# Mask phase of a two-layer cross-attention kernel: the crossbar transfers of the probabilities go from ACT's queue to SP's, one for each head

## What is computed

```python
xq = layer_norm(x, qn_w, qn_b); ctx = layer_norm(context, cn_w, cn_b)
q = (xq @ q_w).reshape(B, N, H, D)                       # H = 16 heads of D = 32
k, v = (ctx @ kv_w) split into keys and values
attn = jnp.einsum('bnhd,bmhd->bhnm', q, k) * scale
attn = softmax(jnp.where(xa_mask, neg, attn))
out = jnp.einsum('bhnm,bmhd->bnhd', attn, v).reshape(B, N, C)
x = x + (out @ proj_w + proj_b)
```

## Time and profile before

| | |
|---|---|
| median of 3 runs | 2843.61 us (2843.58 to 2844.65) |
| the profiled execution | 2851.42 us, its span 2849.7 us |
| mean granted TensorE clock in it | 0.974 |
| busy in the span: PE, DVE, ACT, POOL | 2657.4, 2004.7, 1561.3, 935.0 us |
| DMA queue of SP (q1), of ACT (q10) | 201.66 MB, 33.56 MB |

### The profile page before, as it was taken

One profiled execution on the slowest core, in us unless ns is written; L12 is line 12 of the kernel. 1 busy time (PEld: TensorE's weight loads), 2 busy tenths in 40 slices (PEclk: granted clock), 3 DMA queues, 4 the chain that ended last, 5 costly groups with the idle time before them and its releaser, 6 DMA issues.

```text
span 2849.7 us, 67083 instructions
## 1 busy us (share of the span) xinstructions
PE 2657.4 (93%) x23144; PEld 2268.0 (80%) x23144; DVE 2004.7 (70%) x5443; ACT 1561.3 (55%) x4742; POOL 935.0 (33%) x1033
## 2 busy tenths in 40 slices
PE   6888888788789999999999999999999999999997
PEld 5666667666668888888888888888878888888886
DVE  5777777777665344444346888888788888888887
ACT  5656656565552111111125777777766767676764
POOL 4555545455410000000000333333333434343422
PEclk8999999999999999999999999999999999999999
DMA  5545555564542111211122111111232222222210
GB/s 168 131 116 143 124 121 147 120 148 103 139 124 76 45 50 38 59 44 44 59 74 82 45 45 51 44 44 44 91 99 74 81 72 83 71 84 68 87 51 23
DMA packets 313621, 236.11 MB, mean 83 GB/s; under 512 B 150736, under 2 KB 240848, under 8 KB 312656
## 3 DMA queue, kind: packets, MB, share of 16 engines
q1 hardware_dynamic: 180432, 201.66, 22.5%
q10 hardware_dynamic: 133120, 33.56, 7.0%
HBM read 137.65 MB, written 63.96 MB: 71 GB/s over the span
## 4 chain that ended last, share of the span: by engine, by line
PE 71%; ACT 11%; issue 8%; DVE 8%; ACTq 1%; DMA 1%; POOL 0%; DVEq 0%; POOLq 0%
PE cross_work L181 16%; PE mlp_acc L3287 12%; PE mlp_f L3269 12%; PE causal_work L181 9%; ACT mask_prob_even L948 3%; PE cross_scores L2284 3%; ACT mask_prob L948 3%; PE cross_scores L2261 2%; PE cross_attended L2314 2%; PE causal_scores L2284 2%; DVE mask_cT_lo L1486 2%; PE causal_scores L2261 2%; DVE mask_scores L1548 2%; PE causal_attended L2314 1%; PE mask_scores L2261 1%
## 5 line engine op out<-in xcount | busy, mean ns | idle before, releaser
L3062 ACT ACTIVATE mlp_h<-mlp_f,mlp_b1col 128x512 f32<-128x512 f32 x128 | 88.3, 690 | 525.9 <-PE mlp_f L3269 525.9
L3269 PE MATMUL mlp_f<-mlp_xT_hi,mlp_w 128*128 128x512 f32 x1024 | 335.4, 389 | 0.0
L3169 DVE CAST mlp_hT_hi<-mlp_h 128x512 fp32r<-128x512 f32 x128 | 58.2, 454 | 369.9 <-ACT mlp_h L3062 369.7
L3287 PE MATMUL mlp_acc<-mlp_w,mlp_hT_hi 128*128 128x512 f32 x1024 | 315.2, 389 | 0.0
L948 ACT ACTIVATE cross_prob<-cross_scores,cross_low 128x256 f32<-128x256 f32 x512 | 237.1, 490 | 63.6 <-DVE cross_low L1542 63.6
L948 ACT ACTIVATE causal_prob<-causal_scores,causal_low 128x128 f32<-128x128 f32 (+1 forms) x512 | 210.2, 436 | 93.7 <-DVE causal_low L1548 93.7
L1548 DVE CUSTOM_DVE_ANT_0 mask_scores<-mask_scores,mask_mask 128x256 f32<-128x256 f32 x512 | 200.8, 454 | 75.9 <-PE mask_scores L2261 65.8
L3269 PEld LDWEIGHTS mlp_f<-mlp_xT_hi,mlp_w 128*128 128x128 f32 x1024 | 192.2, 188 | 40.5 <-issue 0.4
L3287 PEld LDWEIGHTS mlp_acc<-mlp_w,mlp_hT_hi 128*128 128x128 f32 x1024 | 192.3, 188 | 39.8
L181 PE MATMUL causal_work<-causal_xT_hi,causal_w 128*128 128x256 f32 x1008 | 217.0, 293 | 0.3 <-DVE causal_qk_parts L1498 0.3
L3269 PE MATMUL mlp_f<-mlp_xT_lo,mlp_w 128*128 128x512 f32 x512 | 199.2, 389 | 0.0
(11 more groups left out here) (368 smaller groups left out, 8295.3 us busy)
## 6 DMA issues: line engine op xcount, KB each, us to landing
cross_x_in<-after_attention SPq DMA_DIRECT2D x17, 512.0 KB, 4.1
mask_x_in<-in_x SPq DMA_DIRECT2D x16, 512.0 KB, 5.7
mask_c_in<-in_ctx SPq DMA_DIRECT2D x16, 512.0 KB, 6.6
mask_res<-in_x SPq DMA_DIRECT2D x16, 512.0 KB, 5.5
after_attention<-mask_res SPq DMA_DIRECT2D x16, 512.0 KB, 2.8
mlp_x<-after_attention SPq DMA_DIRECT2D x8, 1024.0 KB, 5.5
mlp_stage<-in_L_xattn_fc_w SPq DMA_DIRECT2D x8, 1024.0 KB, 5.5
after_layer<-mlp_y SPq DMA_DIRECT2D x8, 1024.0 KB, 4.4
```

Of the source, the lines that this page charges most:

```text
L3062: act.activation(h32[:, m % 2, :], F1[m % 2][:], ACT.Gelu, bias=b1col[:, m:m + 1]).then_inc(s["gelu"], 1)
L3269: ins = pe.matmul(F1[m % 2][:], W[2 * (m // 4)][:, a, k, m % 4 * P:(m % 4 + 1) * P], xT[p][:, k, :], start=(k == 0 and n == 0), stop=(k == ...
L3287: ins = pe.matmul(ACC[t][:], hT[a][:, m % 2, t * P:(t + 1) * P], W[2 * (m // 4) + 1][:, p, m % 4, :], start=(m == 0 and n == 0), stop=(m = ...
```

## The change

Each crossed head is a transfer of its own: four of 256 KB a chunk in place of two of 512 KB. `P16` and `PT16` are laid out by head. The transfers are issued by SP, in a new `cross_over(b, c)`: for chunk 0 after `normed_by_quads(b+1)` and before `load_rows(b+2)`, for chunk 2 after `store(b-1)`. Each waits for the low half of its head. POOL's low halves are one instruction a head (eight a turn in place of four), and those of chunk 2 wait for DVE's last `turned(b+1, k)` (`t_lo`). ACT's `cross_over` is gone; the exps of a crossed chunk wait for the low halves that read the buffer before. Some steps are put elsewhere:

- ACT: `values(b, 0)` after `exps(b, 0)` and `exps(b, 1)`; `qk(b, 2)` before `exps(b, 7)`; `values_middle` before the copies; `high_halves(b, 2, 0)` after `exps(b, 9)`; `qk(b+1, 0)` before `exps(b, 14)`.
- DVE: `turn_over(b+1, 3)` before `minima(b, 2)` and `project(b, 0)` behind them; `qk_lo(b, 3)` after the four `turned(b+1, k)`.
- POOL: `gain` of all four and then all `turned_hi`; `values_low` between the first two gains.

```diff
-        PT16 = r("probT_parts", [P, 2, 2, 2, TT, TT, P], F16)
+        PT16 = r("probT_parts", [P, 4, 2, TT, TT, P], F16)
...
-        P16 = r("prob_parts", [P, 2, 2, 2, TT * S], F16)
+        P16 = r("prob_parts", [P, 4, 2, TT * S], F16)
@@ -489,6 +489,15 @@
             hold(sp, s["out_ready"], b + 1, s)
             sp.dma_start(tokens(dst, b), (res if masked_ctx else y)[:]).then_inc(stored, IT)
 
+        def cross_over(b, c):
+
+            if c >= 2 or not isinstance(b, int) or b > 0:
+                hold(sp, s["av_done"], KC * b + c - 1, s)
+            for h in range(HC):
+                hold(sp, s["p_low"], 8 * b + 2 * c + h + 1, s)
+                sp.dma_start_transpose(PT16[:, h].rearrange("p a q k s -> p (a q k) s"),
+                                       P16[:, h].rearrange("p a n -> p (a n)")).then_inc(s["probs_turned"], IT)
+
         def load_matrix(i):
             if i >= 3 and cross:
 
@@ -567,8 +576,11 @@
             if masked_ctx and nxt:
                 load_mask(b + 1)
                 normed_by_quads(b + 1)
-                if not after:
-                    yield ROOM
+            crossing = masked_ctx and not (isinstance(b, int) and b == B)
+            if crossing:
+                cross_over(b, 0)
+            if masked_ctx and nxt and not after:
+                yield ROOM
             if cross:
                 if after:
                     rows_by_quads(b + 2)
@@ -585,6 +597,8 @@
                 yield ROOM
             if not cross and prev:
                 store(b - 1)
+            if crossing:
+                cross_over(b, 2)
 
         sp.sem_inc(stored, 1)
         sp.sem_inc(s["res_free"], 1)
@@ -667,11 +681,13 @@
             pool.tensor_copy((cT if k // 2 else xT)[0][:, 2 * (k % 2):2 * (k % 2) + 2, :], t32[k // 2][:, k % 2]
                              ).then_inc(s["t_hi"], 1)
 
-        def low_halves(b, c, i):
-
-            pool.wait_ge(s["p_high"], 4 * b + c + i + 1)
-            pool.tensor_tensor(P16[:, i, 1], probs(b, c)[:, 2 * i:2 * i + 2].rearrange("p u t s -> p u (t s)"),
-                               P16[:, i, 0], ALU.subtract).then_inc(s["p_low"], 1)
+        def low_halves(b, c):
+
+            for i in range(2):
+                pool.wait_ge(s["p_high"], 4 * b + c + i + 1)
+                for u in range(2):
+                    pool.tensor_tensor(P16[:, 2 * i + u, 1], probs(b, c)[:, 2 * i + u].rearrange("p t s -> p (t s)"),
+                                       P16[:, 2 * i + u, 0], ALU.subtract).then_inc(s["p_low"], 1)
 
         def values_left(b):
 
@@ -769,25 +785,23 @@
                 if not cur:
                     yield ROOM
                     return
-                low_halves(b, 0, 0)
-                low_halves(b, 0, 1)
+                low_halves(b, 0)
                 values_left(b)
                 if nxt:
                     gain(b + 1, 0)
-                    gain(b + 1, 1)
-                    if not prev:
-                        values_low(b)
-                    gain(b + 1, 2)
                 if prev or not nxt:
                     values_low(b)
                 if nxt:
-                    turned_hi(b + 1, 0)
-                    turned_hi(b + 1, 1)
+                    gain(b + 1, 1)
+                if not prev:
+                    values_low(b)
+                if nxt:
+                    gain(b + 1, 2)
                     gain(b + 1, 3)
-                    turned_hi(b + 1, 2)
-                    turned_hi(b + 1, 3)
-                low_halves(b, 2, 0)
-                low_halves(b, 2, 1)
+                    for k in range(NP):
+                        turned_hi(b + 1, k)
+                    pool.wait_ge(s["t_lo"], NP * (b + 2))
+                low_halves(b, 2)
                 return
             if causal:
                 if cur:
@@ -941,6 +955,8 @@
             c, h = u // HC, u % HC
             if crossed(c):
                 act.wait_ge(s["lifted"], UNITS // 2 * b + HC * (c // 2) + h + 1)
+                if h == 0 and (c >= 2 or not isinstance(b, int) or b > 0):
+                    act.wait_ge(s["p_low"], 8 * b + 2 * c)
             else:
                 act.wait_ge(s["masked"], UNITS * b + u + 1)
             for qt in range(TT):
@@ -962,18 +978,10 @@
         def high_halves(b, c, i):
 
             if i == 0 and (c >= 2 or not isinstance(b, int) or b > 0):
-                act.wait_ge(s["probs_turned"], 2 * IT * (2 * b + c // 2))
+                act.wait_ge(s["probs_turned"], HC * IT * (2 * b + c // 2))
             act.wait_ge(s["exp_done"], UNITS * b + HC * c + 2 * i + 2)
-            act.activation(P16[:, i, 0], probs(b, c)[:, 2 * i:2 * i + 2].rearrange("p u t s -> p u (t s)"), ACT.Copy
+            act.activation(P16[:, 2 * i:2 * i + 2, 0], probs(b, c)[:, 2 * i:2 * i + 2].rearrange("p u t s -> p u (t s)"), ACT.Copy
                            ).then_inc(s["p_high"], 1)
-
-        def cross_over(b, c, i):
-
-            if i == 0 and (c >= 2 or not isinstance(b, int) or b > 0):
-                act.wait_ge(s["av_done"], KC * b + c - 1)
-            hold(act, s["p_low"], 4 * b + c + i + 1, s)
-            act.dma_start_transpose(PT16[:, i].rearrange("p a u q k s -> p (a u q k) s"),
-                                    P16[:, i].rearrange("p a u n -> p (a u n)")).then_inc(s["probs_turned"], IT)
 
         def values_high(b):
 
@@ -1035,9 +1043,9 @@
         def mask_turn(b, prev, cur, nxt):
 
             if cur and prev:
-                values(b, 0)
                 exps(b, 0)
                 exps(b, 1)
+                values(b, 0)
             if prev:
                 pair_kept(b, -1)
             if cur and prev:
@@ -1062,16 +1070,14 @@
 
             exps(b, 4)
             exps(b, 5)
-            cross_over(b, 0, 0)
             exps(b, 6)
+            qk(b, 2)
             exps(b, 7)
-            qk(b, 2)
-            cross_over(b, 0, 1)
+            if prev:
+                values_middle(b)
             copy(b, 4)
             copy(b, 5)
             copy(b, 6)
-            if prev:
-                values_middle(b)
             if not nxt:
                 yield ROOM
                 yield ROOM
@@ -1082,13 +1088,14 @@
             if not nxt:
                 yield ROOM
 
-            for u in (8, 9, 10):
-                exps(b, u)
+            exps(b, 8)
+            exps(b, 9)
+            high_halves(b, 2, 0)
+            exps(b, 10)
             exps(b, 11)
             qk(b, 3)
             if not prev:
                 values_middle(b)
-            high_halves(b, 2, 0)
             high_halves(b, 2, 1)
             pair_kept(b, 0)
             if not nxt:
@@ -1096,14 +1103,14 @@
 
             exps(b, 12)
             exps(b, 13)
-            cross_over(b, 2, 0)
+            if nxt and prev:
+                qk(b + 1, 0)
             exps(b, 14)
             exps(b, 15)
             if not prev:
                 matrix_hi(3)
-            if nxt:
+            if nxt and not prev:
                 qk(b + 1, 0)
-            cross_over(b, 2, 1)
             copy(b, 12)
             copy(b, 13)
             copy(b, 14)
@@ -1713,27 +1720,30 @@
             if nxt and prev:
                 turn_over(b + 1, 1)
                 turn_over(b + 1, 2)
+                turn_over(b + 1, 3)
             if not nxt:
                 yield ROOM
                 yield ROOM
-            if prev:
-                project(b, 0)
+                if prev:
+                    project(b, 0)
 
             minima(b, 2)
             if nxt and prev:
-                turn_over(b + 1, 3)
+                project(b, 0)
             over_sums(b, 0)
             if not prev:
                 turn_over(b + 1, 0)
                 turn_over(b + 1, 1)
             if not nxt:
                 yield ROOM
-            qk_lo(b, 3)
+            if not prev or not nxt:
+                qk_lo(b, 3)
             if not prev:
                 turn_over(b + 1, 2)
             if nxt and prev:
                 for k in range(NP):
                     turned(b + 1, k)
+                qk_lo(b, 3)
             elif nxt:
                 turn_over(b + 1, 3)
                 turned(b + 1, 0)
@@ -2318,7 +2328,7 @@
 
         def attend_parts(b, c):
 
-            pe.wait_ge(s["probs_turned"], 2 * IT * (2 * b + c // 2 + 1))
+            pe.wait_ge(s["probs_turned"], HC * IT * (2 * b + c // 2 + 1))
             if c == 0:
                 pe.wait_ge(s["v_low"], b + 1)
             at = S * (c % 2)
@@ -2327,7 +2337,7 @@
                     for h in range(HC):
                         ins = pe.matmul(O[h * DH:(h + 1) * DH, at:at + S],
                                         VP[v][:, kt, c % KC // 2, h * DH:(h + 1) * DH],
-                                        PT16[:, h // 2, a, h % 2, :, kt, :],
+                                        PT16[:, h, a, :, kt, :],
                                         start=(kt == 0 and n == 0), stop=(kt == 1 and n == len(PARTS16) - 1))
             ins.then_inc(s["av_done"], 1)
 
@@ -3135,7 +3145,7 @@
```

(2 more changed lines are left out.)

## The result

The changed kernel takes 2733.35 us (median of four runs, 2732.44 to 2736.35) against 2844.13 us before (four runs, 2843.58 to 2847.7): ratio 0.961, 95% interval 0.9593 to 0.9626, 111 us less. The forecast was 2740.0, faster. The profiled execution has a span of 2730.4 us; the one before, 2849.7 us, stood 7.8 us above its median, so the two traces differ by 119 us.

What follows compares the result with a forecast made beforehand. No engine full; a chain of hand-overs bounds the mask phase. 7.0 us a turn over 14 turns (98) plus 6 outside gave 104 off the 2843.6 us median: 2740, range 2705 to 2768 (72%).

Steps and rivals of the forecast that it cites:

- The stalls: On ACT's queue, issuing the second crossbar transfer of a chunk delays the copies TensorE awaits: 4.9 us in the mean turn.
- The lo parts: DVE's `cT_lo` subtractions run slowly beside POOL's low halves, 5.16 us in a turn; alone the two would take 1.4 us.
- Rival A's second form: Only the issue stalls go (69 us, 2775) and the DVE gain is eaten by DVE's exposed front; rival A whole 17%.
- SP's queue: Four 256 KB transfers hold it 1.4 us each; chunk 2 lands at 38.9, wanted at 41.0, so not late.
- by bytes: Queue time follows bytes: a 512 KB pair holds its queue 1.87 + 3.76 us and moves as many bytes as four small ones.
- Stretch 4: Loop turn, chunk 3's scores to the next turn's: 8.6 us against 15.3, gain 6.7, with the 1.98 us stall and `cT_lo`.
- the deductions: Taken off the turn's gain: 1.2 us for remaining idle spans and the clock, 0.9 us for hand-overs counted as zero.
- stretch 1: Loop turn, chunk 0's scores to chunk 1's: 11.3 us, gain about -0.2, as DVE's front is no longer hidden.
- stretch 2: Loop turn, chunk 1's scores to chunk 2's: 9.9 us against 13.1, gain 3.2, as no issue stands before the copies.
- stretch 3: Loop turn, chunk 2's scores to chunk 3's: 10.2 us against 10.9, gain 0.7, with ACT last.
- The reordering: On ACT, first exps ahead of `values(b,0)`: gain 1.1 - 1.3 us, nothing net, paying for the cover of DVE's front that goes.
- Rival B: Slower, SP's queue becomes the chain: at 4.3 us a transfer chunks land late, 9.1 us a turn, 2971; chance 7%.

Runs made afterwards that it cites:

- e3: The kernel before with its two 512 KB transfers a chunk issued by SP at the new places and exps waiting for low halves; no order or size changed: 2769.1 us.
- e6: The kernel before with only POOL's low halves of chunk 2 waiting for DVE's last lo part; ACT still issues: 2798.9 us.
- e9: The kernel before with the edits of e3 and e6 together, in the old orders of ACT, DVE and POOL: 2716.5 us.
- e5: The changed kernel with transfers halved once more, eight of 128 KB a chunk: 2759.5 us.
- e7: The changed kernel with values(b,0) and pair_kept(b,-1) ahead of exps(b,0) on ACT: 2727.1 us.
- e10: The kernel of e9 with four 256 KB transfers a chunk and a low half for each head: 2723.0 us.
- e8: e7 with pair_kept(b,0) ahead of chunk 2's second high half and, in turn 0, its first high half back behind values_middle: 2709.1 us.
- e2: The changed kernel with its four small transfers a chunk issued by ACT again, two between the exps and two before the copies: 2858.9 us.

## Why the prediction was right

**The stalls.** The step "both waits are the issuing of the second transfer" held: 4.9 us a turn, 69 us in 14 turns and 6 outside, 75 us by the forecast; e3 took 77.

**The lo parts.** 1.4 us alone, 5.2 beside POOL, forecast 3.8 us a turn, 53 us; e6 took 47, and the rows after show 683 ns. e9 shows that the two parts add up, so neither hides the other. Rival A's second form, in which the lo parts are eaten by the exposed front, falls with it.

**SP's queue.** Taken 1.4 us a transfer and chunk 2 landed 2.1 us before its use. Measured 1.26 us in the median, four in 5.76 us, landing 3.4 us after its issue; in turns 2 to 13 the last landing of chunk 2 is 1.1 to 1.7 us ahead of `attend`, of chunk 0 2.9 to 3.5 us. The reason "by bytes" held for the step that was taken, from 512 to 256 KB: 1 MB holds the queue for 5.08 us in two and 5.76 in four. It fails below: from 256 to 128 KB the price of one transfer hardly falls, and a change that cut them finer would have missed by it, as e5 shows. The Trainium skill (DMA: Bandwidth & Descriptors, "Anatomy of one DMA") gives a part that does not shrink with the size, for GpSimd's path. On SP's queue the rows agree in kind below 256 KB; the estimate of 2.6 us a transfer that the prediction worked out from it is about twice what they have, and the lateness of 1.2 us a turn did not come.

**The four stretches.** Stretch 4 (8.6 forecast, 8.5 measured) and the sum (40.0, then 42.1 with the deductions, 40.9 measured) are right. The parts are less so: 1.5 us too little in stretch 1, 1.1 too much in stretch 2, 0.6 too little in stretch 3. That they nearly cancel, and that the deductions of 2.1 us cover the 0.9 that is left, is in part luck.

Stretch 1 failed: 11.3 forecast, 12.8 measured. Up to `turn_sums` the layout held: `ot` was laid to end at T = 7.9 and ends at 330.56 + 0.62 - 323.12 = 8.1. What I missed is the clock behind it. TensorE stands idle for 2.10 us before `turn_sums` at 331.32, and then (columns of the earlier trace rows):

```profile
331.30:334.70 3.40, 3.38 (x13) 2.79 (x14) 1.18 (x2) 3.40 (x11) 2.31 (x3) 0.67 0.83 309
```

0.67 is a mixture of the levels of 2.4 and 1.2 GHz; `values(b,1)` takes 4.5 us in place of 2.9. Ten of turns 1 to 14 are so. In the four others (6, 9, 12 and 14) the same wait of 2.1 us stands there and the clock stays at its upper level, as in turn 6:

```profile
289.88:293.20 3.32, 3.32 (x17) 2.54 (x17) 1.12 (x2) 3.32 (x11) 2.24 (x3) 1.00 0.85 316
```

Stretch 1 then takes 11.5 us, near the forecast. But stretches 2 and 3 take 9.8 and 11.6 in place of 8.5 and 10.6, and the turn 41.4 us in place of 40.7. All of TensorE's waits shown above for exps (3.3 us in 8) and for `res` (1.7 us in 4) lie in these four turns. So the clock explains stretch 1 and not the turn: a TensorE that comes early waits in the next two stretches. In e7, at 1.00 in all turns but the first, it is the same. The 1.2 us a turn that I took off for the clock therefore stands for no loss that the rows show, though the mean clock came out as supposed (0.97). 7.0 us a turn was forecast, 8.3 came.

**The reordering** of stretch 1, "costed at nothing net", and the others with it were wrong in sign: the new orders cost 10 us (e10). With the first exps ahead of `values(b,0)` TensorE waits 2.1 us for `ot` each time, in e10 0.8 to 1.0 us or not at all, while ACT had stood idle for 4.4 us just before. e7 takes that wait away. In turn 0, `high_halves(b, 2, 0)` ahead of `values_middle` makes ACT wait for the landing of chunk 0, and TensorE stands still at `attended`:

```profile
58.65 0.62 PE L2338 MATMUL mask_attended<-mask_probT_parts,mask_v_part 128*32 128x256 f16 x8 [12.53 <-POOL all_values_low L700]
```

e8 brings that stretch back from 22.0 to 15.8 us. The forecast had 3 us gained in each outer turn; turn 0 lost 2.3 us and the end gained 6 (14.3 - 8.3).

So 111 us are 77 from the issuing, 47 from POOL's wait (sum 124, 129 in e9), less 10 for the orders and some 6 between e9 and e10 for size and single low halves, which the intervals don't part from zero. Rival B, slower through SP's queue, was priced from d = 3.2 us a transfer on; it is 1.3 to 1.4. Its sum has a slip: the gain put back, 7.0 and 0.9, is 7.9 and not 8.1, which would make it 2974 and not 2971.

What stays open is why the second transfer of a pair holds ACT's queue for so long (2.9 to 4.6 us at 256 KB in chunk 0 of e2), when the four on SP follow one another in 1.4 us. In the kernel before, the second hold of a pair ends close to the landing of the first: in turns 2 to 13 0.3 to 0.6 us after it in chunk 0, and from 0.6 before to 0.2 after it in chunk 2. No run tests that apart.

## What to carry to other kernels

Idle time of an engine with no releaser, just behind a DMA that it issues itself, was that DMA's issuing here: try it on a queue that nobody waits for, and count what that queue then holds up. Where one instruction takes some four times its shortest time beside another engine's long one, a wait that keeps the two apart can be worth more than the overlap. When the wait that bounds a loop goes, look through the orders again from the new bound: here the new orders cost 10 us against the old ones, and `ot` first, with one order of turn 0 put back, gave the next 24 us. And a low clock beside a late stretch need not be a loss: the turns at the full clock were the longer ones.

## What the runs showed of the hardware that was not expected

Issuing a crossbar transfer from SP takes about the same at 128 and at 256 KB (8 in 10.62, 4 in 5.76 us: 1.3 and 1.4 us each) and 2.5 us at 512 KB in the mean of two that follow one another (5.08 us). A chunk of 1 MB holds the queue about as long in two pieces as in four, and twice as long in eight. On ACT's queue the same 256 KB took 1.26 us or, as the second of a pair, up to 4.6 us (e2). The lo parts of DVE beside POOL's low halves took 2616 to 2624 ns when a POOL instruction covered two heads (2.4 to 2.6 us long) and 1641 to 1653 ns when it covered one (about 1.5 us there, 1.2 us alone), as if each had to wait for one POOL instruction and then ran in its own 0.7 us, or less where it came in the middle. The Trainium skill (SBUF — State Buffer, section "Who interferes with whom") says that a DVE instruction with two SBUF inputs contends with a GpSimd one that reads SBUF, and that what they contend for is "an exclusive lock"; the step from 2.6 to 1.65 us as the POOL instruction is halved agrees with that, and so do the minima, with one input in PSUM, which take 0.46 us in the median beside the same POOL work and without it.
